# Four triangle-multiplication layers on one core: another arithmetic for the last stages' variance, residual tiles loaded in the triangle stage, another order of layer 3's projection

## The reference

```python
xn = layernorm(group_norm(x))                       # layer 3: group_norm(x) alone
left  = (xn @ Wl) * sigmoid(xn @ Wlg) * mask
right = (xn @ Wr) * sigmoid(xn @ Wrg) * mask
out_gate = sigmoid(xn @ Wog)
t = einsum('bikd,bjkd->bijd', left, right)          # layers 2, 3: 'bkjd,bkid->bijd'
x = x + (layernorm(t) * out_gate) @ Wout            # layers 1, 3: (layernorm(t) @ Wout) * out_gate
```

## Time and profile before

| | |
|---|---|
| time, median of 3 runs | 1606.09 us (1603.01 to 1614.1) |
| the profiled execution | 1603.74 us |
| its span | 1601.5 us |
| busy: PE, DVE, ACT, POOL | 84%, 60%, 61%, 32% of the span |
| mean DMA rate | 156 GB/s |

### The profile page before, as it was taken

One profiled execution on the slowest core, in us unless ns is written; L12 is line 12 of the kernel. 1 busy time (PEld: TensorE's weight loads), 2 busy tenths in 40 slices (PEclk: granted clock), 3 DMA queues, 4 the chain that ended last, 5 costly groups with the idle time before them and its releaser, 6 DMA issues. The chain is left out here.

```text
span 1601.5 us, 43585 instructions
## 1 busy us (share of the span) xinstructions
PE 1345.6 (84%) x12950; PEld 875.4 (55%) x12950; DVE 962.2 (60%) x2784; ACT 973.4 (61%) x2093; POOL 514.8 (32%) x490
## 2 busy tenths in 40 slices
PE   0899997898899989899609999998897666798987
PEld 0455553676454457577406666675664322475665
DVE  6577773388699962177607888213666777511555
ACT  0677773598677751299607888225776777522654
POOL 0455550254565530044306666002332000000333
PEclk9999998899799999999858999998998999998999
DMA  7011114487333325578783332456996333254999
GB/s 262 31 50 49 50 53 131 123 255 228 101 107 108 108 81 148 153 237 256 198 195 100 118 118 98 124 151 184 291 308 205 120 119 122 79 156 143 288 303 275
DMA packets 206500, 249.30 MB, mean 156 GB/s; under 512 B 29024, under 2 KB 196320, under 8 KB 206432
## 3 DMA queue, kind: packets, MB, share of 16 engines
q1 hardware_dynamic: 206432, 248.42, 51.6%
HBM read 139.83 MB, written 108.53 MB: 155 GB/s over the span
## 5 line engine op out<-in xcount | busy, mean ns | idle before, releaser
L974 DVE SCALAR_TENSOR_TENSOR lr<-ps,mask,act_out 128x128 f32 (+5 forms) x1152 | 276.2, 311 | 86.3 <-ACT act_out L724 81.0
L498 PE MATMUL ps<-w_parts,val 64*128 64x256 bf16 (+1 forms) x2112 | 230.5, 304 | 71.1 <-DVE lr L974 69.9
L1127 POOL TENSOR_TENSOR rstd<-ve,half_col 128x6 f32<-128x6 f32 x144 | 190.5, 1323 | 257.6 <-DVE ve L947 223.9
L1171 POOL TENSOR_TENSOR new_ring<-val,res_ring 128x384 f32<-128x384 f32 x96 | 95.9, 1000 | 479.0 <-DVE val L1061 422.2
L724 ACT ACTIVATE act_out<-ps 128x384 f32<-128x384 f32 x384 | 176.1, 483 | 50.5 <-PE ps L508 28.7
L615 PEld LDWEIGHTS ps<-k,sq 128*128 128x128 f32 x1152 | 162.0, 195 | 51.5 <-issue 3.0
L1160 POOL TENSOR_TENSOR val<-act_out,gate_ring 128x384 f32<-128x384 f32 x96 | 96.2, 1002 | 278.8 <-ACT act_out L802 214.4
L498 PEld LDWEIGHTS ps<-w_parts,val 64*128 64x128 bf16 (+1 forms) x2112 | 90.2, 111 | 166.5 <-DVE lr L974 124.8
L1040 DVE TENSOR_TENSOR xn<-ps,cen 128x384 f32<-128x384 f32 x192 | 107.1, 558 | 105.3 <-PE ps L623 104.5
L768 ACT ACTIVATE in_ring<-ps 128x768 f32<-128x768 f32 (+1 forms) x64 | 51.9, 812 | 183.0 <-PE ps L566 166.2
L608 PE MATMUL ps<-in_ring,k 128*128 128x384 f32 x288 | 133.4, 550 | 28.8 <-DMA in_ring<-t_scratch 28.6
(11 more groups left out here) (99 smaller groups left out, 2493.8 us busy)
## 6 DMA issues: line engine op xcount, KB each, us to landing
gate_scratch<-gate_ring SPq DMA_DIRECT2D x192, 192.0 KB, 2.3
gate_ring<-gate_scratch SPq DMA_DIRECT2D x96, 384.0 KB, 3.9
in_ring<-x_scratch SPq DMA_DIRECT2D x144, 192.0 KB, 2.4
in_ring<-t_scratch SPq DMA_DIRECT2D x144, 192.0 KB, 4.5
res_ring<-x_scratch SPq DMA_DIRECT2D x72, 384.0 KB, 5.0
x_scratch<-new_ring SPq DMA_DIRECT2D x48, 384.0 KB, 3.3
t_scratch<-in_ring SPq DMA_DIRECT2D x48, 384.0 KB, 2.7
lr<-x SPq DMA_DIRECT2D x6, 1536.0 KB, 15.6
```

The lines of the kernel that those rows point to most:

```text
L498: mm = nc.tensor.matmul(banks[h][:, :, 0:P], moving(x, s)[half(h), N * r:N * r + P], proj_weights(w, h)[:, 0:2 * P], start=start, stop=sto ...
L974: ins = nc.vector.scalar_tensor_tensor(out5[:, h, lo // 2:hi // 2, :, m], ps[:, 4 + 2 * r + h, lo:hi].rearrange("p (a e) -> p a e", e=2), ...
L1127: nc.gpsimd.tensor_tensor(rstd[:, s % 2, :], ve[:, s % 2, :], half_col[:, :], ALU.pow)\
```

## The change

1. In the last stage of every layer the sum of squares is taken from two bf16 parts. PE does six bf16 matmuls for a tile, with `sel_bf`, where it did three float32 ones. DVE gets a new step `square_low(n + 4)` (one `tensor_tensor` of 128 x 384 with both inputs in SBUF), first in its turn. PE now waits for it (`b2_sq_lo`).
2. The residual tiles of layers 1 to 3 are no longer loaded into `res_ring` in the last stage. They are loaded into parts of `lr` in the triangle stage, as soon as the groups that used these parts are done (`freed_slots`): in layers 2 and 3 one pair of tiles after each even group and two after each odd one; in layer 1 two after each odd group up to 7, then one after each even and three after each odd one. One semaphore counts all; the reader waits once, for all of them.
3. In layer 1 SP no longer waits for `b2_new` in its turn.
4. In layer 3's stage A both rows are projected wide first, then narrow, and each row waits for its own `a_free` at its start.

```diff
@@ project(n, s, r) on PE
-                    if r == 0:
+                    if r == 0 or not ln:
                         pe.wait_ge(a_free, l * SUBS + m + 1)
...
-                            if r == 0 and stop:
+                            if ln and r == 0 and stop:
                                 pe.wait_ge(a_free, l * SUBS + m + 2)
...
-                    if r == 0:
+                    if r == 0 or not ln:
                         wide()
                         mm = narrow()
@@ phase_b1 on SP, at the end of each group
+                    for n in freed_slots(l, g) if l else []:
+                        sp.dma_start(slots[:, RES_SLOT[l] + n:RES_SLOT[l] + n + 2, :], two_tiles(x_src(l), n))\
+                            .then_inc(res_loaded, 16)
@@ phase_b2 on SP
-                    if l:
-                        load_res(n, n)
...
-                    sp.wait_ge(b2_new, l * TILES + n + 1)
                     if l != 1:
+                        sp.wait_ge(b2_new, l * TILES + n + 1)
...
-                    if l and ahead >= RING:
-                        load_res(n - 1 + RING, s - 1)
@@ phase_b2 on PE
-                    pe.wait_ge(b2_sq, base + n + 1)
+                    pe.wait_ge(b2_sq_lo, base + n + 1)
                     for j in range(CHUNKS):
-                        mm = nc.tensor.matmul(ps[:, 6 + s % 2, 2 * j:2 * j + 2],
-                                              sq[:, s % 2, P * j:P * j + P], k_sel, start=True, stop=True)
+                        for part in (sq_high, sq_low):
+                            mm = nc.tensor.matmul(ps[:, 6 + s % 2, 2 * j:2 * j + 2],
+                                                  part[:, s % 2, P * j:P * j + P], sel_bf[:, :],
+                                                  start=part is sq_high, stop=part is sq_low)
@@ phase_b2 on DVE
+                def square_low(n, s):
+                    dve.wait_ge(b2_sq, base + n + 1)
+                    nc.vector.tensor_tensor(sq_low[:, s % 2, :], sq[:, s % 2, :], sq_high[:, s % 2, :],
+                                            ALU.subtract).then_inc(b2_sq_lo, 1)
                 def step(n, i, s, ahead):
+                    if ahead >= 4:
+                        square_low(n + 4, s)
                     if ahead >= 3:
                         inverse(n + 3, (s + 3) % RING)
...
+                elif l:
+                    dve.wait_ge(res_loaded, 16 * TILES // 2 * l)
@@ phase_b2 on POOL
-                    pool.wait_ge(res_loaded[s // 2], 16 * ((l - 1) * TURNS + i + 1))
...
-                    nc.gpsimd.tensor_tensor(new_ring[:, s, :], val[:, s % 2, :], res_ring[:, s, :], ALU.add)\
+                    nc.gpsimd.tensor_tensor(new_ring[:, s, :], val[:, s % 2, :], residual_slot(l, n), ALU.add)\
+                else:
+                    pool.wait_ge(res_loaded, 16 * TILES // 2 * l)
```

More of the change, by code:

```diff
@@ L56 @@
 GATE_FIRST = (True, False, True, False)
+RES_SLOT = (None, 48, 32, 32)
 T_SCALE = (1.0, 1.0, 1.0 / N, 1.0)
@@ L79, in build_triangle_layers @@
         in_ring = sb("in_ring", [P, RING, TILE])
-        res_ring = sb("res_ring", [P, RING, TILE])
         gate_ring = sb("gate_ring", [P, RING, TILE])
@@ L140, in build_triangle_layers @@
         in_loaded, gate_stored = sems("in_loaded"), sems("gate_stored")
-        t_loaded, res_loaded, gate_loaded, new_stored = (
-            sems(name, PAIRS) for name in ("t_loaded", "res_loaded", "gate_loaded", "new_stored"))
+        t_loaded, gate_loaded, new_stored = (
+            sems(name, PAIRS) for name in ("t_loaded", "gate_loaded", "new_stored"))
+        res_loaded = sem("res_loaded")
         planes_stored = sems("planes_stored", 2)
@@ L163, in build_triangle_layers @@
             sem("b2_" + s) for s in ("z", "cen", "sq", "var", "std", "rstd", "rb", "bc", "zn"))
+        b2_sq_lo = sem("b2_sq_lo")
         b2_aff, b2_val, b2_out, b2_gated, b2_new, b2_turned = (
@@ L195, in column_parts, with x_parts, residual_slot @@
             return [tile.rearrange("p (r h i) -> p h r i", h=2, r=ROWS)[:, h, :, :] for h in range(2)]
-        def x_parts(l, ring, s):
+        def x_parts(l, tile):
             if l != 2:
-                return [ring[:, s, :]]
-            return [ring[:, s, :].rearrange("p (h r i) -> p h r i", h=2, r=ROWS)[:, h, :, :] for h in range(2)]
+                return [tile]
+            return [tile.rearrange("p (h r i) -> p h r i", h=2, r=ROWS)[:, h, :, :] for h in range(2)]
+        slots = lr[:, :].rearrange("p (a f) -> p a f", f=TILE)
+        def residual_slot(l, n):
+            return x_all[:, n, :] if l == 0 else slots[:, RES_SLOT[l] + n, :]
+        def freed_slots(l, g):
[4 more added lines that the diff above has]
+            return [n for n in pairs if n < TILES]
         def two_tiles(dram, n):
@@ L333, in load_gate @@
                     sp.dma_start(gate_ring[:, s:s + 2, :], two_tiles(gate_dram, n)).then_inc(gate_loaded[s // 2], 16)
-                def load_res(n, s):
-                    sp.dma_start(res_ring[:, s:s + 2, :], two_tiles(src, n)).then_inc(res_loaded[s // 2], 16)
                 def gate_used(n):
@@ L451, in centre @@
                     for z, x in zip(column_parts(l, ps[:, s % 2, 0:TILE]),
-                                    x_parts(l, in_ring, s) if l else [x_all[:, n, :]]):
+                                    x_parts(l, in_ring[:, s, :]) if l else [x_all[:, n, :]]):
                         mm = nc.tensor.matmul(z, w_centre[:, :], x, start=True, stop=True)
@@ L1046, in finish @@
                     if GATE_FIRST[l]:
-                        if l:
-                            dve.wait_ge(res_loaded[s // 2], 16 * ((l - 1) * TURNS + i + 1))
-                        res = x_parts(l, res_ring, s) if l else [x_all[:, n, :]]
+                        res = x_parts(l, residual_slot(l, n))
                         slot_free(dve, new_stored[s // 2], 16 * (l // 2 * TURNS + i))
@@ L1078, in step @@
                         finish(n + lead, i + (s + lead) // RING, (s + lead) % RING)
+                square_low(0, 0)
+                square_low(1, 1)
                 inverse(0, 0)
+                square_low(2, 2)
                 inverse(1, 1)
@@ L1084, in phase_b2 @@
                 inverse(2, 2)
+                square_low(3, 3)
                 if lead:
                     finish(0, 0, 0)
+                elif l:
+                    dve.wait_ge(res_loaded, 16 * TILES // 2 * l)
                 over_tiles(dve, step)
```

## The result

The changed kernel takes 1526.84 us (median of 4 runs, 1522.89 to 1531.67) against 1608.65 of the kernel before in the same session: ratio 0.949, 95% interval 0.945 to 0.954. The forecast was 1552; the direction holds, the size is 25 us short, and the time lies just 2 us inside the fast end of the range (1525 to 1602) and 3 outside the band of the forecast case (1530 to 1566). The profiled execution took 1531.67 us, its span 1529.5, so the span fell by 72 us.

What follows compares the result with a forecast made beforehand. ACT was taken to bound layer 0's last stage, PE layer 1's, DMA layers 2 and 3, a chain of waits layer 3's stage A. +6 - 7 - 18 - 24 + 8 - 22 + 3 = -54 gave 1552 us, range 1525 to 1602.

Steps and rivals of the forecast that it cites:

- forecast case: Whole kernel: the outcome with none of the rivals, 1530 to 1566 us, chance 0.58.
- What bounds the kernel: Last stages: ACT bounds layer 0 (1.95 us a tile), PE layer 1 (2.29), DMA layers 2 and 3 (2.63, 2.56).
- Layers 0 and 2 and the port: Last stages: DVE becomes latest at 2.07 and 2.23 us a tile, +6 and -18 us; +3 for tiles where POOL is first.
- A near tie: Layers 0 and 2: POOL starts 1.55 to 1.65 us after the reciprocal, the new instruction 1.57 to 1.65 and 1.7 to 1.8.
- Layer 1, -7: Last stage: PE 1.85, ACT 2.15, DVE 2.16, taken as 2.14 us a tile: -7 us, bounds -10 to -2.
- Layer 3, -24: Last stage: four engines close together, 2.02 us a tile over 45 tiles: -24 us, bounds -29 to -16.
- Triangle stage and starts, +8: Added loads cost +5 us in layer 1, +1.5 each in layers 2 and 3: +8 us, bounds 0 and +20.
- 292 to 304 is all this queue gave: Triangle stage: DMA queue rate capped at 292 to 304 GB/s, so layer 1's 344 GB/s costs some 5 us.
- Layer 3's projection, -22: Stage A: a loop once in two tiles sets 2.78 us a tile instead of 3.24: -22 us, bounds -32 to -11.
- port rival: POOL takes the port first in layers 0 and 2: 2.88 us a tile, about 1617 us; chance 0.10, one layer 0.14.
- DMA rival: Triangle stages become DMA-bound at 260 GB/s, 73 us instead of 64: 1571 us; chance 0.14 shared with the clock.
- granted clock: Layer 0's last stage: PE rests more and may drop to 1.2 GHz, up to +45 us; chance 0.14 shared with DMA.

Runs made afterwards that it cites:

- res_only: Kernel before with only the residual of layers 1 to 3 loaded in the triangle stage (SP's `b2_new` wait gone in layer 1): 1577.48 us, ratio 0.986.
- load_again: Changed kernel, with layers 2 and 3's residual pairs loaded a second time in the last stage into a ring nothing reads: 1570.89 us, 0.979 of the kernel before.
- var_only: Kernel before with only the last stages' variance taken from two bf16 parts, `square_low` first in DVE's turn: 1595.43 us, ratio 0.995.
- proj_only: Kernel before with only layer 3's projection changed, each row wide first with its own wait: 1577.68 us, ratio 0.985.
- order_only: Changed kernel with layer 3's old single wait for both banks restored, both rows still wide first: 1548.04 us, 0.966 of the kernel before.
- pad_ahead: Changed kernel with two DVE memsets into an unread tile ahead of `square_low` in layers 0 and 2: 1584.43 us, 0.986 of the kernel before.
- res_double: Changed kernel with every residual pair loaded twice in the triangle stages of layers 2 and 3, second copy unread: 1555.27 us, 0.967 of the kernel before.

## Why the prediction was right, and what was mis-sized

- *What bounds the kernel.* Right, and shown: PE in layer 1 and DMA in layers 2 and 3 with PE close behind. `res_only` brings layers 2 and 3 to just PE's 2.3 us, `load_again` brings DMA's bound back. That ACT bounds layer 0 wasn't tried by itself: PE is at 79.37 of 80 there, ACT at 77.97.
- *Layers 0 and 2 and the port, +6 - 18 + 3 = -9.* Measured +9.5 - 19.2 = -9.7, by errors that cancel: luck. DVE's free turn is 1.98 in layer 0, not 2.07, and 2.11 in layer 2, not 2.23: some 4 and 5 us less. The port took 9.9 and 5.1 us, 15 instead of 3. In layer 0 the turn before was 1.92 once the stage ran (the 1.95 of the sum holds some of the slower first tiles), so that the last 40 turns grew by 11.0 us, 2.4 from the free turn and 8.6 from the port, and the first seven shrank by 1.7. The step that failed is the size of the port's term. "A near tie" was right; +3 was a mean over cases with nothing under it, and it leaned on the gate load to hold POOL back. That helps only where the load is last: in layer 2 16 of the 43 tiles in which the two met waited for it, and POOL won none of these; in layer 0 it was never last.
- *Layer 1, -7.* Measured -12, beyond my bounds of -10 to -2: 2.03 a tile against my 2.14. ACT is busy 75.00 of 75 and DVE 74.26, which fits the engines that I named, though PE is at 74.70 too and no run tells the three apart. The step that failed is their need, 2.15 and 2.16, taken from busy times: busy time in an engine with rests holds the ends of instructions that stand alone, and back to back each of them overlaps the next by 0.07 to 0.1 us (341.00 + 0.54 against 341.47 above). That this is the whole reason is argued, not tried. The move of the residual helped here too, which the forecast didn't say: in `var_only` layer 1's DMA is at 0.96 and ten of its tiles take over 2.5 us (102.5 against 95.0). SP's wait, which went away with it, was not tried by itself.
- *Layer 3, -24.* -28.2. An undisturbed turn takes 1.87, but others are longer, and the mean over the stage is 2.00 (94.2 over 47), as good as the 2.02 forecast. What is beyond -24 is that 47 turns gained 0.56 each, not 45, and that the end behind the last reciprocal is 1.5 us shorter (8.9 to 7.4).
- *Triangle stage and starts, +8.* Measured +1.5 in the stages, and even that isn't the loads': layer 3's took 62.8 us from PE's first product to its last before and 64.3 after, but 64.3 also in `var_only` and `proj_only`, which don't have the new loads, and 62.8 in `order_only` and `load_again`, which do. From PE's last triangle product to the first reciprocal it went from 17.7, 16.0 and 18.0 us to 19.1, 18.2 and 17.8 in layers 1 to 3, which the last stages' figures above contain. Of this only layer 1's +1.4 stands out (17.1 to 17.7 in the runs without the new loads, 19.1 and more in those with them); layer 2's start took 18.3 and 18.8 in `var_only` and `proj_only`. So some 1 to 2 us are shown, not 8, and layer 1, where I feared for the stage's length, kept it. The step that failed is "292 to 304 is all this queue gave": those rows come from last stages, and the triangle stage's transfers run up to 376.
- *Layer 3's projection, -22.* -23.2; 2.80 a tile against 2.78. In the new trace PE's projection (L511) waits for `glu`, its weight loads 67 times between 1240 and 1335, as the loop of the forecast has it, and `order_only` shows that the wait counts; the loop's other links weren't tried.
- *Sum.* -54 forecast, -72 in the spans; 7 more of the 25 us because the median lies 4.8 below the profiled execution here, and I had put it 2.4 above. Every group of terms but that of layers 0 and 2 erred to the slow side, and this carried the time out of the forecast case.
- *Rivals.* The port rival's tile of 2.88 was real: 2.85 in `pad_ahead`, which it takes 0.23 us of delay to reach. The DMA rival didn't come, and the granted clock was 0.98 to 1.00 in the four last stages.

## What to carry to other kernels

Where two resources stand close (in layer 2 PE needed 2.40 of DMA's 2.63 us a tile), price the parts of a change as a set: here the two gained 31 us one by one and 55 together. Where a two-SBUF-input instruction of VectorE can start within 0.1 us of a large GpSimd one, don't leave it to chance: put the engine with slack second. A tiny instruction ahead of its large one did that here. Before an instruction is moved within its engine's turn, look at what stands behind its reader on the reader's engine.

## What the runs showed of the hardware

- Which of the two gets the port isn't decided by the record's start alone. POOL ahead by 0.01 us lost (340.99 and 341.00), ahead by 0.09 it won (342.90 and 342.99). Between these there is no sharp line: in the changed kernel's layer 2 it was ahead by 0.04 to 0.06 in ten tiles, and won three. A 128 x 6 GpSimd instruction 0.07 ahead didn't lengthen `square_low` (0.55, line of 345.58).
- The loser ends sooner behind the winner than its own length would have it. A blocked DVE instruction ended 0.42 behind POOL's end (its own length 0.54), a blocked POOL one 0.86 behind DVE's (345.66 + 1.33 against 345.58 + 0.55; its own length 1.00): 0.12 to 0.14 less than the own length in both.
- In these runs a DMA share over 1.0 went with a bound, and GB/s alone told less: 1.06 went with 311 GB/s in layer 3's last stage and 1.07 with 376 in the triangle stage of `res_double`. Mean packets (23.41 MB in 14527 before in a last stage, 20.11 MB in 19265 there) were larger where the rate was lower, so their size isn't the reason; what is stays open.
- Why it is each fourth tile of layer 0 in which POOL comes early isn't shown either. In four turns in a row POOL starts 0.06 and 0.11 behind DVE, then 0.01 and 0.09 ahead, and the lost turn begins the round again. It has the period of the ring's four slots.
